# Gathering six queries at a time and picking each row's query with diagonal masks on TensorE, in the attention pass of a graph network

## The reference

```python
q = (h @ Wq + bq).reshape(n, HD, HEADS) * scaling
k = (h @ Wk + bk).reshape(n, HD, HEADS)
v = (h @ Wv + bv).reshape(n, HD, HEADS)
s = jnp.einsum('edh,edh->eh', q[rows], k[cols])
m = jax.ops.segment_max(s, rows, num_segments=n)
e = jnp.exp(s - m[rows])
z = jax.ops.segment_sum(e, rows, num_segments=n)
attn = e / z[rows]
out = jax.ops.segment_sum(attn[:, None, :] * v[cols], rows, num_segments=n)
return out.reshape(n, -1) @ Wo + bo
```

## Time and profile before

| | |
|---|---|
| three runs | 5511.86, 5547.48, 5551.34 us; median 5547.48 |
| the profiled execution | 5550.51 us, its span 5548.5 us |
| granted TensorE clock, mean | 0.554 of full speed |
| busy: PE, DVE, ACT, POOL | 1140.2, 3339.7, 1173.7, 3490.6 us |
| the attention pass | from about 3968 to 5427 us of the span |
| DMA, mean over the span | 187 GB/s, 1039.53 MB |

### The profile page before, as it was taken

One profiled execution on the slowest core, in us unless ns is written; L12 is line 12 of the kernel. 1 busy time (PEld: TensorE's weight loads), 2 busy tenths in 40 slices (PEclk: granted clock), 3 DMA queues, 4 the chain that ended last, 5 costly groups with the idle time before them and its releaser, 6 DMA issues. The chain is left out here.

```text
span 5548.5 us, 25079 instructions
## 1 busy us (share of the span) xinstructions
PE 1140.2 (21%) x4115; PEld 749.2 (14%) x4115; DVE 3339.7 (60%) x6732; ACT 1173.7 (21%) x2663; POOL 3490.6 (63%) x3686
## 2 busy tenths in 40 slices
PE   4333321105222221006222200019500000000005
PEld 3222221104111110004111100016300000000003
DVE  7766676644444443436345432337488889888996
ACT  4222222222222222224222222225200000000001
POOL 4666566665666666665676676653476666666653
PEclk7555555557555555557555555559755555555557
DMA  5555455554555655556555565553576777677753
GB/s 177 182 173 169 158 184 173 185 184 138 199 185 189 204 188 189 185 184 187 196 195 195 198 205 174 186 177 128 164 227 211 215 217 219 210 216 222 218 182 106
DMA packets 325740, 1039.53 MB, mean 187 GB/s; under 512 B 71351, under 2 KB 124740, under 8 KB 292172
## 3 DMA queue, kind: packets, MB, share of 16 engines
q0 software_dynamic: 209408, 628.59, 37.8%
q1 hardware_dynamic: 116172, 409.34, 19.9%
HBM read 649.96 MB, written 388.11 MB: 187 GB/s over the span
## 5 line engine op out<-in xcount | busy, mean ns | idle before, releaser
L533 POOL DMA_INDIRECT G<-tab,ix x2349 | 2236.7, 952 | 1146.0 <-issue 692.1
L559 DVE SCALAR_TENSOR_TENSOR G<-tail,pass_lists,G 128x256 f32<-128x256 f32 x1566 | 698.5, 479 | 1218.2 <-DMA G<-tab,ix 529.4
L1678 POOL DMA_INDIRECT kv<-kvtab,dst_ix x936 | 888.6, 949 | 429.2 <-issue 279.4
L597 ACT ACTIVATE tail<-G 128x512 f32<-128x512 f32 x783 | 470.6, 601 | 1607.6 <-issue 637.7
L599 ACT ACTIVATE wide<-G 128x256 f32<-128x256 f32 x783 | 299.8, 383 | 947.5 <-DVE G L559 498.7
L673 PE MATMUL tail<-weights,hT 128*128 128x256 f32 x588 | 304.9, 673 | 754.8 <-issue 453.5
L559 DVE SCALAR_TENSOR_TENSOR G<-wide,pass_lists,G 128x256 f32<-128x256 f32 x783 | 374.5, 478 | 100.0 <-issue 77.4
L1867 PE MATMUL trio<-ident,state 128*128 128x128 f32 x6 | 2.0, 430 | 1474.3 <-DVEq L1889 1474.3
L673 PEld LDWEIGHTS tail<-weights,hT 128*128 128x128 f32 x588 | 172.4, 324 | 837.7 <-issue 481.6
L1727 DVE TENSOR_TENSOR kv<-kv,wide 128x3072 f32<-128x3072 f32 x78 | 260.9, 3344 | 28.7 <-DMA kv<-kvtab,dst_ix 28.7
L1743 DVE TENSOR_REDUCE s<-kv 128x96 f32<-128x3072 f32 x78 | 260.9, 3345 | 0.0
(11 more groups left out here) (343 smaller groups left out, 3634.4 us busy)
## 6 DMA issues: line engine op xcount, KB each, us to landing
hist<-G SPq DMA_DIRECT2D x261, 1152.0 KB
G<-tab,ix POOLq DMA_INDIRECT x2349
ahist<-state SPq DMA_DIRECT2D x78, 408.0 KB
tab<-o SPq DMA_DIRECT2D x147, 128.0 KB
kv<-kvtab,dst_ix POOLq DMA_INDIRECT x936
h<-tab SPq DMA_DIRECT2D x98, 128.0 KB
G<-tab SPq DMA_DIRECT2D x98, 128.0 KB
kvtab<-okv SPq DMA_DIRECT2D x49, 256.0 KB
```

What stands on the lines that cost most here:

```text
L533: g.indirect_dma_start(G[b][:, k, :], None, tab, bass.IndirectOffsetOnAxis(ix[:, b, k:k + 1], 0)).then_inc(s_eg[b].sem, 16)
L559: ins = v.scalar_tensor_tensor(out=G[b][:, k, :], in0=state2 if c == 2 else state[:, c, :], scalar=reset[:, at:at + 1], in1=G[b][:, k, :], ...
L597: a.activation(state, of[:, 0:2, :], ACT.Copy).then_inc(c_state.sem, 1)
L1678: g.indirect_dma_start(kvs[n % KB][:, k, :], None, kvtab, bass.IndirectOffsetOnAxis(dst_ix[:, at:at + 1], 0)).then_inc(s_kv[n % KB], 16)
```

## The change

A window is now six steps long (`T` = 6, 13 windows), and there are two query buffers. POOL fetches the queries of the next window in the last three steps of a window, one lane in each, 128 pieces of six queries of 1 KB (L1677 of the new kernel).

The first query of a window is no longer copied by ACT, and DVE copies nothing. DVE writes once a window, for each row of it, which of the six queries it needs, as zeros and a one (`choose`, after `maximum` of a window's second step; new line L1708). ACT makes from each such column of numbers a 128x128 mask: the identity matrix, scaled in each partition by the zero or one (L1826). PE multiplies mask by queries and adds up in PSUM (`pick`, L1850): in step `t` of a window a row can need the queries 0 to `t`, so there are 3(t+1) picks of 128x256, and as many masks, except that step 0 uses the identity itself. That makes 3, 6, 9, 12, 15, 18 picks in the six steps. Each pick raises `c_picked` and each mask `c_mask` by one. A step's picks wait for the multiply before, since both use the same place in PSUM, and the multiply waits for all picks of its step. The masks of a step are made one step ahead, in front of that step's exponential; there are 15 mask buffers, and a mask waits until the pick that used its buffer is done.

The second query buffer and nine of the masks lie where 18 of the node tiles of `X` are. SP saves these 18 tiles to `tab` in DRAM (2.36 MB) among the `later` loads of the last `project`, and brings them back in `carry_attention` (new line L1971), which waits for them.

```diff
@@ -39,3 +39,3 @@
 STEPS = J // C
-T = 3
+T = 6
 UB = 3
@@ -121,3 +121,3 @@
     NOROW = P * RP
@@ -1631,5 +1631,10 @@
         def attention_pass(st, state, empty):
-            KB, QB = 4, 3
+            KB, QB, MASKS = 4, 2, 15
             kvs = [sb(st, f"kv{b}", [P, SLOT * R, KV]) for b in range(KB)]
-            qs = [sb(st, f"q{b}", [P, R, T, D]) for b in range(QB - 1)] + [next_queries]
+            whole = sb(st, "q", [P, R, T, D])
+            qs = [[whole[:, r, :, :] for r in range(R)], [next_queries] + [X[:, r * T:(r + 1) * T, :] for r in range(R - 1)]]
+            more = X[:, (R - 1) * T:LENT - 1, :].rearrange("p t (m f) -> p (t m) f", f=P)
+            masks = mask_room + [more[:, m, :] for m in range(MASKS - len(mask_room))]
+            which = X[:, LENT - 1, 0:QB * R * T * T].rearrange("p (q r t j) -> p q r t j", q=QB, r=R, t=T)
+            number = X[:, LENT - 1, QB * R * T * T:QB * R * T * T + T]
             s = sb(st, "s", [P, SLOT + 1, R, HEADS])
@@ -1639,3 +1644,3 @@
             pairs = pass_lists[:, 0:2 * R * D].rearrange("p (a r f) -> p a r f", a=2, r=R)
-            c_query, c_scored, c_passed = sem("att_query"), sem("att_scored"), sem("att_passed")
+            c_scored, c_which, c_mask, c_picked = sem("att_scored"), sem("att_which"), sem("att_mask"), sem("att_picked")
             s_query = [sem(f"att_q{b}") for b in range(QB)]
@@ -1643,5 +1648,2 @@
             WINDOWS = NBA // T
-            one_on = wide[:, R * D:R * D + R * WINDOWS * 2].rearrange("p (r w j) -> p r w j", r=R, j=2)
-            two_on = wide[:, R * D + R * WINDOWS * 2:R * D + R * WINDOWS * 3].rearrange("p (r w) -> p r w", r=R)
             query = wide[:, 0:R * D].rearrange("p (r f) -> p r f", f=D)
@@ -1659,2 +1661,12 @@
+            used = [picks + 1 for picks in range(NBA * R * (T + 1) // 2) if picks % (R * T * (T + 1) // 2) >= R]
+            def picks(n):
+                return R * (n // T * (T * (T + 1) // 2) + (n % T) * (n % T + 1) // 2)
+            def masked(n):
+                return picks(n) - R * -(-n // T)
             with block() as blk:
@@ -1663,6 +1675,5 @@
                     def queries(window, r):
-                        if window < WINDOWS:
-                            at = r * WINDOWS + window
-                            g.indirect_dma_start(qs[window % QB][:, r, :, :].rearrange("p t f -> p (t f)"), None, qtab_flat,
-                                                 bass.IndirectOffsetOnAxis(win_ix[:, at:at + 1], 0)).then_inc(s_query[window % QB], 16)
+                        at = r * WINDOWS + window
+                        g.indirect_dma_start(qs[window % QB][r].rearrange("p t f -> p (t f)"), None, qtab_flat,
+                                             bass.IndirectOffsetOnAxis(win_ix[:, at:at + 1], 0)).then_inc(s_query[window % QB], 16)
@@ -1678,5 +1689,7 @@
                             g.indirect_dma_start(kvs[n % KB][:, k, :], None, kvtab, bass.IndirectOffsetOnAxis(dst_ix[:, at:at + 1], 0)).then_inc(s_kv[n % KB], 16)
-                        if i + 1 >= QB:
-                            g.wait_ge(c_passed, 1 + i + 1 - QB + 1)
-                        queries(i + 1, b)
+                        window, t = divmod(n, T)
+                        if t >= T - R and window + 1 < WINDOWS:
+                            if window:
+                                g.wait_ge(c_picked, picks(window * T))
+                            queries(window + 1, t - (T - R))
                     staged(g, NBA, UB, [(0, gather)])
@@ -1686,2 +1699,4 @@
                     chain.link(v.memset(state[UB - 1][:, :, :], 0.0))
+                    for t in range(T):
+                        chain.inc(v.memset(number[:, t:t + 1], float(t)))
                     ranks = row_rank.rearrange("p (w t) -> p w t", t=T)
@@ -1689,5 +1704,7 @@
                     offs = off[:, :, :].rearrange("p (r w) t -> p r w t", r=R)
-                    chain.inc(v.tensor_scalar(one_on, offs[:, :, :, 1:T], 1.0, None, ALU.is_ge))
-                    v.tensor_scalar(two_on, offs[:, :, :, 2], 2.0, None, ALU.is_ge).then_inc(c_passed, 1)
-                    v.wait_ge(c_passed, 1)
+                    def choose(window):
+                        v.tensor_tensor(which[:, window % QB, :, :, :], offs[:, :, window, :, None].to_broadcast([P, R, T, T]),
+                                        number[:, None, None, :].to_broadcast([P, R, T, T]), ALU.is_equal).then_inc(c_which, 1)
+                    choose(0)
@@ -1705,23 +1722,14 @@
-                    def pass_on(i, b):
-                        if b == UB - 1:
-                            return
-                        q = qs[i % QB]
-                        v.wait_ge(c_query, times(i, b, 1) + 1)
-                        if b == 0:
-                            keep("query", i * UB + 1, v.copy_predicated(query, one_on[:, :, i, 0:1].bitcast(I32).to_broadcast([P, R, D]), q[:, :, 1, :]))
-                        else:
-                            chain.link(v.copy_predicated(query, one_on[:, :, i, 1:2].bitcast(I32).to_broadcast([P, R, D]), q[:, :, 1, :]))
-                            v.copy_predicated(query, two_on[:, :, i:i + 1].bitcast(I32).to_broadcast([P, R, D]), q[:, :, 2, :]).then_inc(c_passed, 1)
+                    def next_window(i, b):
+                        window, t = divmod(i * UB + b, T)
+                        if t == 1 and window + 1 < WINDOWS:
+                            if window:
+                                v.wait_ge(c_mask, masked(window * T))
+                            choose(window + 1)
                     def multiply(i, b):
-                        keys = kvs[(i * UB + b) % KB][:, :, 0:D].rearrange("p (e r) f -> p e r f", r=R)
-                        if b == 0:
-                            v.wait_ge(c_query, times(i, b, 1))
-                        elif b == 1:
-                            waits("query", i * UB + b)
-                        else:
-                            v.wait_ge(c_passed, i + 2)
-                        v.wait_ge(s_kv[(i * UB + b) % KB], ((i * UB + b) // KB + 1) * (16 * GATHERS))
+                        n = i * UB + b
+                        keys = kvs[n % KB][:, :, 0:D].rearrange("p (e r) f -> p e r f", r=R)
+                        v.wait_ge(c_picked, picks(n + 1))
+                        v.wait_ge(s_kv[n % KB], (n // KB + 1) * (16 * GATHERS))
                         v.tensor_tensor(keys, keys, query[:, None, :, :].to_broadcast([P, SLOT, R, D]), ALU.mult).then_inc(c_scored, 1)
@@ -1801,3 +1809,3 @@
                     staged(v, NBA, UB, [(0, multiply), (2, put_second), (1, weigh(0)), (0, add_up), (1, weigh(1)), (0, before), (0, block_empty), (1, hold),
-                                        (0, maximum), (0, pass_on), (1, pair), (0, top), (1, put_z), (0, differ), (1, put_first)])
+                                        (0, maximum), (0, next_window), (1, pair), (0, top), (1, put_z), (0, differ), (1, put_first)])
@@ -1805,10 +1813,18 @@
                 def _(a):
-                    def bring(i, b):
-                        if b == 0:
-                            a.wait_ge(s_query[i % QB], (i // QB + 1) * (16 * R))
-                        if is_first(i, b):
-                            a.wait_ge(c_passed, 1)
-                        if not is_first(i, b):
-                            a.wait_ge(c_scored, times(i, b - 1, 1))
-                        a.activation(query, qs[i % QB][:, :, 0, :], ACT.Copy).then_inc(c_query, 1)
+                    def mask(i, b):
+                        n = i * UB + b
+                        if n >= NBA:
+                            return
+                        window, t = divmod(n, T)
+                        if t == 1:
+                            a.wait_ge(c_which, window + 1)
+                        for m in range(R * (t + 1) if t else 0):
+                            r, j = divmod(m, t + 1)
+                            made = masked(n) + m
+                            if made >= MASKS:
+                                a.wait_ge(c_picked, used[made - MASKS])
+                            a.activation(masks[made % MASKS], ident[:, :], ACT.Copy, scale=which[:, window % QB, r, t, j:j + 1]).then_inc(c_mask, 1)
+                    def mask_ahead(i, b):
+                        mask(i, b + 1)
@@ -1817,3 +1833,21 @@
                         a.activation(wts[b], w[:, b, :, :, :], ACT.Exp).then_inc(c_e.sem, 1)
-                    staged(a, NBA, UB, [(0, bring), (1, expo)])
+                    staged(a, NBA, UB, [(0, mask_ahead), (0, expo)])
+                @blk.tensor
+                def _(pe):
+                    def pick(i, b):
+                        n = i * UB + b
+                        window, t = divmod(n, T)
+                        if t == 0:
+                            pe.wait_ge(s_query[window % QB], (window // QB + 1) * (16 * R))
+                        if n:
+                            pe.wait_ge(c_scored, n)
+                        for m in range(R * (t + 1)):
```

(26 more changed lines are left out.)

## The result

| | kernel before | changed kernel | ratio, 95% interval |
|---|---|---|---|
| first comparison | 5541.27 us (4 runs) | 5705.32 us (4 runs, 5679.74 to 5708.69) | 1.0283, 1.0256 to 1.0309 |
| once more (`after_again`) | 5535.86 us | 5652.46 us | 1.0206, 1.0170 to 1.0241 |
| once more (`after_third`) | 5528.62 us | 5748.84 us | 1.0427, 1.0366 to 1.0488 |

The change makes the kernel slower by 2 to 4%; the forecast was 5480. Of the four executions of the changed kernel, one in the second row and two in the third are slow by over 1.5% against the fastest beside them; the third row's two others, 5664.01 and 5731.97 us, are 1.025 and 1.037 of the kernel before. The runs fell on chips of two kinds. On the first kind the kernel before takes 5529 to 5541 us, on the other 4928 to 4937. All of this table is of the first kind.

The account below looks back on a forecast made before the run. DVE was taken to bound the pass, by its counts in stalled steps and its work in calm ones, POOL next. DVE -76 and start +5 make -71 from 5550.5: 5480 us, low 5380, high 5740.

Parts of the forecast that it names:

- The counts of PE and ACT: Attention pass: some 20 added semaphore counts a step, beside 15 of DVE, taken to cost 0.
- The third rival: Picks come late, by PE's counts 1.40 us apart in stalled steps or 0.86 us picks: 5527 or 5525 us; chance 20%.
- The second rival: Stalled counts served one engine at a time, so PE's and ACT's come between DVE's: slower, 5690 us; chance 30%.
- DVE: -76 us: Attention pass: without 78 query copies, 27 stalled steps of 21.2 and 50 calm of 15.29 us, 1337 against 1413.
- The model of 48 counts at 1.40 us: Stalled stretch of the pass: three steps in 67.2 us, paced by DVE's 48 counting instructions, 1.40 us each.
- The number of stalled steps: Of the pass's 77 steps, 27 at 22.4 us and 50 calm at 16.12 before; the 27 held fixed after.
- POOL: 0: Attention pass: 12.5 gather issues a step, 15.7 us, under DVE's mean step of 17.4, so 0; 20 us without a lead.
- PE's picks: 0.43 us each, hidden: Between multiplies: 18 picks take 8.1 us in 11.9 us of room at 1.2 GHz, so 0.
- the row x4 of the earlier trace: Profile row read as four 128x256 fp32 products in 2.08 us at 1.2 GHz, speaking against 0.85 us a pick.
- Masks: ACT's 128x128 masks, estimated 477 ns each; eighteen make 8.6 us in a step of 15.29, hidden, 0.
- `choose`: One DVE instruction of 128x108 a window, 0.3 us, adding 0.05 us a step.
- Start and ends: First query gathers +5 us; saving node tiles beside the projection 0, bringing them back in the carry 0, each at most 10.

Follow-up runs that it names:

- before_no_copies_c: Kernel before with DVE's three query copies left out (wrong queries), a repeat on the first kind of chip: 5525.51 us beside 5528.62, ratio 0.9992.
- before_in_pairs: Kernel before with two key-and-value rows fetched by one gather, 7 gathers a step instead of 13: 5358.84 us, ratio 0.9666.
- in_pairs: Changed kernel with two key-and-value rows fetched by one gather, 6 such gathers a step instead of 12, same bytes: 5289.51 us, ratio 0.9541.
- pe_one: Changed kernel, a pick raising its count only at a step's last and once more in six-query steps; other kind of chip: 4875.29 us, ratio 0.9891.

## Why the prediction was wrong

- **The counts of PE and ACT: "I take 0".** This is the step that failed. Thirteen intervals of 37.1 and thirteen of 25.8 us instead of 15.2 are 13 x (21.9 + 10.6) = 422 us. The third rival had the mechanism, PE's counts come late in the busy stretches, but at 1.40 us a count, a pace copied from DVE: nine counts would then have cost nothing. In their place the nine took up to 27 us, the last three of them 4.7 us each, and a single one took 24. What sets that length is shown only in part: the number of gathers and POOL's lead do, PE's own number of counts does not. The second rival, which held the slower side, had the wrong victim: DVE's own counts never were late again. That its figure, 5690, lies near the measured 5705 is luck.
- **DVE: -76 us.** Wrong as well here, and hidden by the first. The copies' 75 us of running and their 65 us of waits were on DVE, which the earlier trace rows shows as the engine that waits, and which is 1245 of 1440 us busy. But taking the copies away left the pass as long as it was (`before_no_copies_c`, 3 us), and 7 gathers a step instead of 13 took 181 us off it (1413 to 1232, `before_in_pairs`): the pass hung on the gathers. The model of 48 counts at 1.40 us fitted one stretch; with 16 counts or 15 a step, the mean step was 18.36 us and 18.33. The number of stalled steps, held fixed at 27, is what moved, as the prediction feared. With half the gathers the term comes out at 68 us.
- **POOL: 0.** On the other kind of chip this is where the gain lay: half a gather a step, 48 us, and the variants with fewer counts got it, 1.1%. On the first kind the same half gather at 1.41 us would be an estimated 54 us; no run there isolates it.
- **PE's picks: 0.43 us each, hidden.** Hidden, yes, but in a window's sixth step with only 0.7 to 2.2 us to spare before the next multiply; the price was misread. The picks after a pause run at the lower of the two clocks, then at the higher. A window of 3.6 us of the third step's picks, after a pause of PE, and one of 6 us in the sixth step of the next window, where PE had been at work since 4196.4:

```profile
3986.50:3990.10 3.60, 3.55 (x8) 2.86 (x9) 3.60 (x2) 0.00 (x0) 2.69 (x3) 0.50 0.68 211
...
4202.00:4208.00 6.00, 5.24 (x24) 4.21 (x22) 6.00 (x12) 0.36 (x2) 0.75 (x1) 0.99 0.00 0
```

  A product of fp32 shows as two instructions, so eight in 3.55 us are four picks, 0.89 each at granted clock 0.50 (1.2 GHz), and 24 in 5.24 us are twelve, 0.44 each, at 0.99. The pass has 819 picks, and PE ran 5753 - 4115 = 1638 instructions more than before. So the row x4 of the earlier trace rows was two products, not four, and did not speak against the four passes. The four passes of the Trainium skill ("FP8 and Floating Point Precision", TensorE Precision Notes), an estimated 0.85 us at 1.2 GHz, agree with this.
- **Masks:** 0.39 us against the estimate of 0.48; nine in a row take 2.72 us, as they overlap. **`choose`:** 0.26 against 0.3. Right.
- **Start and ends:** 0 rather than +5. The first multiply comes 21.53 us after the first gather in both kernels. Saving `X` shows as DMA traffic alone. From the carry's first memset to its first gathered row are 32.6 us in both (before 5430.68 to 5463.30, now 5587.78 to 5620.38), so bringing `X` back costs nothing, as forecast:

```profile
3780.00:3826.00 46.00, 34.81 (x122) 21.59 (x121) 31.19 (x132) 20.60 (x57) 7.97 (x8) 0.85 0.36 129
5588.00:5617.00 29.00, 6.94 (x26) 5.39 (x26) 13.08 (x23) 1.08 (x2) 6.02 (x6) 0.56 0.32 102
```

What stays open: why a count is late at all, and which part of a gather fills what (its 16 counts or its 128 pieces; `in_pairs` halves both), why the last in line is DVE in the kernel before and PE in the changed one, and what makes chips of the two kinds differ. The traces of the first kind hold far fewer records of semaphore updates by DMA than those of the other (16479 in the changed kernel, 70636 in `pe_one`); whether the recording has a part in the lateness no run can tell. That on the other kind the changed kernel itself gains what its variants gain was not run.

## What to carry to other kernels

Before costing a saving on the fullest engine, try what its work is worth by taking some of it away. Here that changed nothing, though DVE was the fullest engine and showed the waits; taking gathers away changed much. A wait for an engine's own earlier instruction can say that counts are late. A change that puts a new engine between two instructions of the old one, with its reply to wait for, then pays for that lateness. Here it paid in two steps of six. Limiting how far the issuing engine may run ahead shortened the waits, and no cost showed on the other kind of chip; fewer counts did not.

## What the runs showed of the hardware

- A count can come 27 us after the work that raises it, while gathers of 128 pieces, issued 1.25 us apart, land; with half as many gathers of twice the size (259 GB/s) no multiply waited. In the same stretch DVE's own counts came in time. The Trainium skill ("TensorE: Matmul & The Clock Gate", The cost: per-tile semaphore tail) gives 26.3 ns for a count of PE; where counts are late the runs are far from it, and where none is late nothing here speaks against it.
- The two kinds of chip differ by 11% for the same kernel (5541 and 4928 us) at nearly the same durations of single instructions: a gather's issue 0.95 us on both, a multiply 3.34.
- DVE's late counts in the kernel before (up to 4.4 us) went away as soon as PE's were the late ones.
